# Row sums of attention: one pair of slabs added on VectorE, two chained to it on POOL, half the sums on TensorE

## The reference

```
h = _sln(hidden, w, ...)                       # layer norm, gain and bias from w
qkv = (h @ Wqkv.T + bqkv).reshape(B, N, num_heads, hd, 3)
energy = jnp.einsum('bhqd,bhkd->bhqk', q, k)
att = jax.nn.softmax(energy, axis=-1) / D ** 0.5
out = jnp.einsum('bhqk,bhkd->bhqd', att, v)
out = out.reshape(B, N, D) @ Wp.T + bp
h1 = out + hidden
return _sln(h1, w, ...) + h1
```

## Time and profile before

| | |
|---|---|
| median of three runs | 1395.69 us |
| the profiled execution | 1395.35 us |
| its span | 1393.7 us |
| mean granted clock of TensorE | 0.979 |
| PE busy | 1331.2 us, 96% |
| DVE busy | 909.3 us, 65% |
| ACT busy | 701.5 us, 50% |
| POOL busy | 984.6 us, 71% |
| sums on PE (L864), busy, both buffers | 110.9 + 16.8 us |
| adds on POOL (L1642), busy, both buffers | 493.4 + 75.7 us |

### The profile page before, as it was taken

How to read it: one execution, slowest core, us unless ns; L and a number is a source line. 1 busy time by engine, 2 the same in 40 slices (tenths; PEclk the granted TensorE clock), 3 DMA queues, 4 the chain that set the end, 5 groups by cost and what they waited for, 6 DMA issues and landing times.

```text
span 1393.7 us, 34891 instructions
## 1 busy us (share of the span) xinstructions
PE 1331.2 (96%) x10948; PEld 928.2 (67%) x10948; DVE 909.3 (65%) x1634; ACT 701.5 (50%) x1374; POOL 984.6 (71%) x755
## 2 busy tenths in 40 slices
PE   6898999999999999999999999999999999999993
PEld 4897676767676767777676767677656555655562
DVE  5345767667676767676776767666666667666535
ACT  4221455555555555555555555555564646565341
POOL 1443175656666688979787888877797969797845
PEclk8899899999999999999999999999999999999997
DMA  7577534443443545645453544626463424253321
GB/s 245 155 209 221 131 93 108 111 106 116 106 115 86 151 107 144 154 124 147 113 159 88 165 118 140 155 77 165 103 168 85 116 80 119 83 137 92 87 56 64
DMA packets 216709, 174.17 MB, mean 125 GB/s; under 512 B 105492, under 2 KB 186516, under 8 KB 216632
## 3 DMA queue, kind: packets, MB, share of 16 engines
q1 hardware_dynamic: 214456, 166.83, 44.7%
q0 software_dynamic: 1984, 6.29, 1.2%
q10 hardware_dynamic: 192, 0.07, 0.0%
HBM read 113.29 MB, written 58.51 MB: 123 GB/s over the span
## 4 chain that ended last, share of the span: by engine, by line
PE 83%; DVE 5%; SPq 4%; issue 3%; DMA 2%; ACT 1%; POOL 1%; DVEq 1%; POOLq 0%; ACTq 0%
PE ps_o L851 15%; PE ps_st L834 15%; PE ps_a L820 12%; PE ps_w L725 10%; PE ps_w L783 9%; PE ps_s L864 8%; PE ps_st L820 4%; PE ps_st L783 3%; DVE half_max L1360 3%; PE ps_w L898 1%; PE ps_w L771 1%; PE ps_s L876 1%; PE ps_s L783 1%; PE ps_o L725 1%; ACT p L1129 1%
## 5 line engine op out<-in xcount | busy, mean ns | idle before, releaser
L1129 ACT ACTIVATE p<-ps_st 128x512 f32<-128x512 f32 x864 | 484.7, 600 | 436.9 <-PE ps_st L834 433.1
L1360 DVE TENSOR_REDUCE half_max<-ps_a 128x1 f32<-128x512 f32 x729 | 484.6, 685 | 256.4 <-PE ps_a L820 254.1
L1642 POOL TENSOR_TENSOR p<-p 128x1024 f32<-128x1024 f32 x208 | 493.4, 2392 | 220.2 <-PE ps_o L851 219.3
L834 PE MATMUL ps_st<-q_stack,k_stack 98*128 98x512 f32 x1024 | 415.7, 408 | 8.4 <-DMA q_stack<-max_rows 4.6
L820 PE MATMUL ps_a<-k_stack,q_stack 96*128 96x512 f32 x729 | 305.8, 421 | 12.7 <-DVE half_max L1360 10.0
L834 PEld LDWEIGHTS ps_st<-q_stack,k_stack 98*128 98x128 f32 x1024 | 195.1, 191 | 72.9 <-ACT p L1129 38.0
L851 PE MATMUL ps_o<-p,v_head 128*32 128x256 f32 x3456 | 209.2, 382 | 0.0
L1360 DVE TENSOR_REDUCE half_max<-ps_st 128x1 f32<-128x512 f32 x231 | 158.3, 685 | 70.7 <-PE ps_st L820 70.7
L820 PEld LDWEIGHTS ps_a<-k_stack,q_stack 96*128 96x128 f32 x729 | 138.0, 190 | 88.0 <-issue 40.8
L783 PEld LDWEIGHTS ps_w<-hT_s,wqkv_s 128*128 128x128 f32 x1056 | 157.2, 190 | 20.1
L851 PEld LDWEIGHTS ps_o<-p,v_head 128*32 128x32 f32 x3456 | 110.1, 110 | 78.4 <-issue 5.0
(11 more groups left out here) (199 smaller groups left out, 1361.7 us busy)
## 6 DMA issues: line engine op xcount, KB each, us to landing
qk_scratch<-qkT_s SPq DMA_DIRECT2D x108, 256.0 KB, 2.4
q_stack<-qk_scratch SPq DMA_DIRECT2D x192, 128.0 KB, 2.6
k_stack<-qk_scratch SPq DMA_DIRECT2D x192, 128.0 KB, 2.8
x_tile<-in_x SPq DMA_DIRECT2D x34, 256.0 KB, 4.9
gq_s<-gain_bias_scratch SPq DMA_DIRECT2D x16, 512.0 KB, 4.3
v_scratch<-v_parts SPq DMA_DIRECT2D x32, 256.0 KB, 3.3
v_head<-v_scratch SPq DMA_DIRECT2D x64, 128.0 KB, 2.1
att_scratch<-o_stage SPq DMA_DIRECT2D x240, 32.0 KB, 1.5
```

The costliest lines, as they stand in the source:

```text
L834: pe.matmul(ps_st[:, (ST_BANK_WIDE if wide else ST_BANK)[2 * k + e], :], k_stack[0:98, s, k * 128:(k + 1) * 128], q_stack[0:98, s, e * 512 ...
L1129: nc.scalar.activation(p_of(step // 8, tiles)[:, k, e * 512:(e + 1) * 512], ps_st[:, (ST_BANK_WIDE if tiles else ST_BANK)[2 * k + e], :], ...
L1360: V.tensor_reduce(half_max[:, s % 2, item:item + 1], A_BANK[bank], AX.X, ALU.max).then_inc(a_used, 1)
L1642: G.tensor_tensor(p[:, slot, :], p[:, slot - 2, :], p[:, slot, :], ALU.add).then_inc(pair_added, 1)
```

## The change

Per half head there were two adds on POOL and two groups of sums on PE. Now the slabs 4h, 4h+1, 4h+2, 4h+3 of half h are joined to one. DVE adds slab 4h to 4h+1 (`slab_add`), when PE's weighted part has read these two (the count of `pv_done` after the first two slabs of the block). POOL adds 4h+2 to 4h+3, when all four are read, and then 4h+1 to 4h+3, when DVE's add and its own first one are done. PE sums slab 3 and slab 7 alone (`chain_sum`). POOL's number of adds stays. `sum_done` counts two a head instead of four.

DVE's adds stand in its order at step 0 (second half of the head before) and at step 4 (first half), behind the reductions, the evacuation and the negated maxima of that step, and ahead of the rest. ACT's waits follow: slab 0 and 4 are free after DVE's add, 2 and 6 after POOL's first, 1 and 5 after POOL's second, 3 and 7 after the sum.

```diff
-        SUM_SLOT = [2, 3, 6, 7]
+        SUM_SLOT = [3, 7]
...
-            def pair_sums(g, s, j, near=False):
+            def chain_sum(g, s, h, near=False):
...
-                pe.wait_ge(pair_added, 16 * g + 4 * s + j + 1)
+                pe.wait_ge(pair_added, 16 * g + 4 * s + 2 * h + 2)
                 for e in range(4):
-                    mm = pe.matmul(ps_s[HD * e:HD * e + HD, 0:QW], root_s[:], p_of(s, near)[:, SUM_SLOT[j], e * QW:(e + 1) * QW],
-                                   start=(j == 0), stop=(j == 3))
+                    mm = pe.matmul(ps_s[HD * e:HD * e + HD, 0:QW], root_s[:], p_of(s, near)[:, SUM_SLOT[h], e * QW:(e + 1) * QW],
+                                   start=(h == 0), stop=(h == 1))
...
-                j = 2 * (k // 4) + k % 2 if paired else k // 2
-                freed = 16 * i + 4 * (step // 8) + j + 1 - 4 * behind
+                half, v = k // 4, 4 * i + step // 8 - behind
+                freed, count = {0: (slab_added, 2 * v + half + 1), 1: (pair_added, 4 * v + 2 * half + 2),
+                                2: (pair_added, 4 * v + 2 * half + 1), 3: (sum_done, 2 * v + half + 1)}[k % 4 if paired else 3]
...
+            def slab_add(g, s, h, near):
+
+                dve.wait_ge(pv_done, 16 * g + 4 * s + 2 * h + 1)
+                p = p_of(s, near)
+                V.tensor_tensor(p[:, 4 * h + 1, :], p[:, 4 * h, :], p[:, 4 * h + 1, :], ALU.add).then_inc(slab_added, 1)
...
+                        if k == 0 and not (first and s == 0) and not (last and s > 0):
+                            slab_add(i - (s == 0), (s - 1) % 4, 1, tiles or (joining and s == 0))
+                        if k == 4 and not last:
+                            slab_add(i, s, 0, tiles)
...
             def pair_add(g, s, j, near=False):
...
+                if j % 2:
+                    pool.wait_ge(slab_added, 8 * g + 2 * s + h + 1)
+                    pool.wait_ge(pair_added, total + j)
+                else:
+                    pool.wait_ge(pv_done, total + 2 * h + 2)
+                G.tensor_tensor(p[:, 4 * h + 3, :], p[:, 4 * h + 2 - j % 2, :], p[:, 4 * h + 3, :], ALU.add).then_inc(pair_added, 1)
```

More of the change, by code:

```diff
@@ L218, in conditioned_attention @@
         pv_done = sem("pv_done")
+        slab_added = sem("slab_added")
         pair_added = sem("pair_added")
@@ L877, in slab_sums @@
                                        start=(k == 0), stop=(k == 7))
-                mm.then_inc(sum_done, 1)
+                if j % 2:
+                    mm.then_inc(sum_done, 1)
             def fin_part(n):
@@ L993, in iteration @@
                                     weighted(*before, j, near=near)
-                            for j in (0, 1):
-                                pair_sums(*before, j, near=near)
+                            chain_sum(*before, 0, near=near)
                             if mode != "bare":
@@ L1002, in iteration @@
                         if k == 4 and behind and (not last or finishing):
-                            for j in (2, 3):
-                                pair_sums(*before, j, near=near)
+                            chain_sum(*before, 1, near=near)
                         if k == 4 and tiles:
@@ L1105, in take_sums @@
             def take_sums(v, s):
-                act.wait_ge(sum_done, 4 * v + 4)
+                act.wait_ge(sum_done, 2 * v + 2)
                 nc.scalar.activation(o_stage[:, s % 2, QW:2 * QW], ps_s[:, 0:QW], ACT.Copy).then_inc(s_taken, 1)
@@ L1126, in exps @@
                     if e == 0:
-                        need(act, pair_added if paired and k not in SUM_SLOT else sum_done, freed)
+                        need(act, freed, count)
                     nc.scalar.activation(p_of(step // 8, tiles)[:, k, e * 512:(e + 1) * 512], ps_st[:, (ST_BANK_WIDE if tiles else ST_BANK)[2 * k + e], :], ACT.Exp
@@ L1319, in last_norm @@
                 dve.wait_ge(pv_done, 4 * NV)
-                dve.wait_ge(sum_done, 4 * NV)
+                dve.wait_ge(sum_done, 2 * NV)
                 dve.wait_ge(att_out[1], ATT_LAST)
@@ L1403, in _, with iteration @@
                     tile_stats(LEAD, step // 3)
-            def iteration(i, mode, norms, outs, first=False, late=True, closing=False):
+            def iteration(i, mode, norms, outs, first=False, late=True, closing=False, joining=False):
                 pair = i - FIRST_OUTS
@@ L1462, in _ @@
             iteration(LAST_TILES - 1, "tiles", False, True)
-            with dve.Fori(LAST_TILES, LAST - 1) as i:
+            iteration(LAST_TILES, "bare", False, True, joining=True)
+            with dve.Fori(LAST_TILES + 1, LAST - 1) as i:
                 iteration(i, "bare", False, True)
@@ L1637, in pair_add @@
             def pair_add(g, s, j, near=False):
-                slot = SUM_SLOT[j]
-                pool.wait_ge(pv_done, 16 * g + 4 * s + 2 * (j // 2) + 2)
+                h, total = j // 2, 16 * g + 4 * s
                 p = p_of(s, near)
-                G.tensor_tensor(p[:, slot, :], p[:, slot - 2, :], p[:, slot, :], ALU.add).then_inc(pair_added, 1)
+                if j % 2:
+                    pool.wait_ge(slab_added, 8 * g + 2 * s + h + 1)
[3 more added lines that the diff above has]
+                G.tensor_tensor(p[:, 4 * h + 3, :], p[:, 4 * h + 2 - j % 2, :], p[:, 4 * h + 3, :], ALU.add).then_inc(pair_added, 1)
             def norm(pair, a):
```

2 lines of the change are left out of this document (1 added, 1 removed).

## The result

The changed kernel takes 1387.26 us (median of four runs, 1385.82 to 1391.84), the kernel before 1395.99 on the same chip: ratio 0.9942, interval 0.9917 to 0.9966. Six more runs gave 1386.39 (e11), ratio 0.9928, interval 0.9913 to 0.9943. The profile called after is of the slowest execution of its four (1391.84), that of e11 of the fastest of its six (1382.51). I had forecast 1402 and slower; it is 0.6% to 0.7% faster. The time lies in the range, but the direction is wrong. It is my second rival (1384) that came about.

A forecast was written before the change was run, and what follows sets the result against it. PE was taken to bound iterations 0 to 9, POOL's path 11 to 14; -15.6 + 0 - 2.9 + 15.7 = -2.8, plus 4 (DVE) and 5 (clock), gave +6: 1402 us, range 1370 to 1418.

The forecast's parts named there:

- my second rival (1384): Whole kernel not slower: POOL loses nearer 0.8 than 1.1 us per add, waits 35 us, giving 1384; chance 0.25.
- PE's gain, 53 us: On PE, each of 120 blocks loses one of two groups of sums, 0.443 us each, 53.2 us in all.
- The exclusion: A DVE op with two SBUF inputs and a POOL op do not run together; whichever comes second waits.
- The loss per add, "where POOL is busy, it loses the full 1.1": Where POOL has no idle time before its adds, each DVE add costs it 1.1 us.
- the turning point at 0.95 a loss: About 0.95 us of POOL loss per add decides between not slower and slower.
- Iterations 5 to 9, forecast 0: POOL's lag adds up; PE waits 3.6 us an iteration against a gain of 3.5: nothing, five times.
- Iterations 11 to 14, forecast +15.7: POOL is level with PE already; PE waits 29.9 us against a gain of 14.2, net loss 15.7.
- the 5 us that I gave the clock: New PE waits in iterations 11 to 14 bring one or two clock falls, 5 us in sum, between none and 12.
- DVE's own waits, +4: DVE waits for POOL's op (0.7 to 1.1 us) in six tight half heads, about 0.7 each, 4 us.
- Iterations 0 to 3, forecast -3.1 each: DVE goes first, POOL starts 0.35 us late; one sum in eight comes 0.4 late, gain 3.1 an iteration.
- +0.4 (10): Iteration 10: PE has one wait of 0.6 us, leaving a gain of 2.9.

The follow-up runs named there:

- e11: The changed kernel unaltered, measured once more in six runs: 1386.39 us, ratio 0.9928 to the kernel before.
- e1: Changed kernel with DVE's add replaced by a reduction of the same length with one SBUF input (slab 4h missing from sums): 1359.61 us, ratio 0.973.
- e2: Changed kernel with no DVE instruction in the add's place, only the count passed on (slab 4h missing from sums): 1362.29 us, ratio 0.9747.
- e3: Changed kernel with POOL's second add of each half left out, DVE's add kept (two slabs missing from sums): 1354.38 us, ratio 0.9696.
- e4: Changed kernel with each group of sums done twice on PE, giving back the removed work: 1429.7 us, ratio 1.0237.
- e9: Changed kernel, but with the form before in iterations 11 to 14 and in three half heads of iterations 5 to 9: 1371.37 us, ratio 0.9822.
- e7: Changed kernel with DVE's add over 512 of the 1024 columns (the other half missing from the sum): 1377.18 us, ratio 0.9866.
- e8: Changed kernel with the form before in three half heads from iteration 4, and in 11 to 14 except three half heads: 1387.74 us, ratio 0.993.
- e10: Changed kernel with DVE's add moved ahead of the reductions of its step: 1603.48 us, ratio 1.148.

## Why the prediction was wrong

**PE's gain, 53 us: right.** Where nothing else holds PE, e1 gives 3.66 us for each of iterations 6 to 8, e2 and e3 3.4, the forecast 3.54.

**The exclusion: right.** What I read from instructions of 256 elements holds at 1024: e1 against the change shows it, and each collision shown here has the same arithmetic. POOL and DVE in iteration 6 after the change:

```profile
616.98 1.29 POOL L1562 TENSOR_TENSOR y_t<-y_t,go_s 128x512 f32<-128x512 f32 x1
618.28 5.79 POOL L1658 TENSOR_TENSOR p<-p 128x1024 f32<-128x1024 f32 x2
...
628.03 1.51 POOL L1549 TENSOR_TENSOR res_t<-res_t,bp_s 128x512 f32<-128x512 f32 x1
...
635.71 0.77 POOL L1523 TENSOR_SCALAR h_tile<-x_tile,std_t 128x512 f32<-128x512 f32 x1 [0.20 <-issue]
636.66 2.04 POOL L1531 TENSOR_TENSOR h_tile<-h_tile,gq_s 128x512 f32<-128x512 f32 x1 [0.18 <-POOL h_tile L1523]
...
646.54 1.58 POOL L1514 TENSOR_TENSOR std_t<-std_t,minus_half 128x1 f32<-128x1 f32 x1
```
```profile
617.73 1.63 DVE L1294 TENSOR_TENSOR p<-p 128x1024 f32<-128x1024 f32 x1
...
627.16 1.22 DVE L1294 TENSOR_TENSOR p<-p 128x1024 f32<-128x1024 f32 x1
...
635.98 1.57 DVE L1294 TENSOR_TENSOR p<-p 128x1024 f32<-128x1024 f32 x1 [0.36 <-PE ps_o L852]
...
646.49 1.23 DVE L1294 TENSOR_TENSOR p<-p 128x1024 f32<-128x1024 f32 x1 [0.78 <-PE ps_o L852]
```

At 617.73 DVE waits for POOL's 1.29 us and ends at 619.36, 1.09 after it; POOL's pair of adds then lasts 5.79 in place of 4.75. Undisturbed, the add took 1.22, the size that I took.

The Trainium skill (SBUF — State Buffer, section Who interferes with whom) says that a DVE instruction with two SBUF inputs contends with a POOL instruction that reads SBUF, and that this sharing is an exclusive lock: one holds it and the other blocks. e1 and the change agree with it, 1359.6 against 1387.3 us. Which of the two blocks is not told by the starts of their records: in e4 DVE's stands first (642.42 against 642.61), and DVE was blocked.

**The loss per add, "where POOL is busy, it loses the full 1.1": the step that failed.** Of the four adds shown above, the first costs POOL 1.0, the second 0.2 (1.51 against 1.29: most of DVE's time lay beside POOL's pause and its DMA), the third 0.8, the fourth 1.0, and that on an instruction of one column (1.58 where its likes take 0.56). The mean over the run is 0.65, and 0.65 over the eight adds of an iteration like this one too (71.39 against the 66.18 us that POOL is busy in iteration 6 of e1). In iteration 13, where it matters most, it is 0.77 (63.34 against 57.18 in iteration 12 before). I had seen POOL's pauses and read them as too short to help (0.68 at most), but the part of an add that lies beside a pause costs POOL nothing, as the second of the four shows. The prediction itself put the turning point at 0.95 a loss; 0.65 and 0.77 lie below it. The rival's own figures were not hit in their parts: PE's waits are 30.8 us where it had 35, and the clock, by the estimate below, took some 6 where it had 2, so that 1384 is met in part by luck.

**Iterations 5 to 9, forecast 0, came out at -1.6 each.** PE's idle time rose from 0.55 (the 79.22 less 78.67 of the earlier trace rows) to 2.13 us, 1.6 in place of my 3.6 of waits.

**Iterations 11 to 14, forecast +15.7, came out at +14.5 and +11.6.** The waits before the sums are 19.0 us in e11 (four of 3.3 to 3.5 for p_far, four of 1.2 to 1.4 for p), where I had 29.9, for the same reason. Less the 14.2 us of fewer sums that makes 4.8 of the 11.6. Most of the other 6.8 is the clock, by the estimate below. (In the prediction I wrote that PE had idled 3.0 us at 1113.08; the row has 2.59.) POOL, PE and the windows there, e11:

```profile
1148.81 3.21 POOL L1658 TENSOR_TENSOR p_far<-p_far 128x1024 f32<-128x1024 f32 x1
```
```profile
1152.08 1.08 PE L865 MATMUL ps_s<-p_far,root_s 128*32 128x256 f32 x8 [3.49 <-POOL p_far L1658]
...
1154.11 0.63 PE L821 MATMUL ps_a<-k_stack,q_stack 96*128 96x512 f32 x1
...
1158.02 0.40 PE L821 MATMUL ps_a<-k_stack,q_stack 96*128 96x512 f32 x1
```
```profile
1152.08:1157.52 5.44, 5.44 (x18) 3.67 (x19) 2.95 (x5) 2.65 (x5) 5.36 (x4) 0.50 0.94 190
1157.52:1166.02 8.50, 8.11 (x63) 4.72 (x61) 8.20 (x14) 6.32 (x13) 8.42 (x5) 1.00 0.20 55
```

PE had idled 3.49 us, and the 5.4 us behind ran at 0.50 (1.2 GHz), products of 512 columns at 0.63 us, then at 1.00 (2.4 GHz) and 0.40. One such stretch holds ten products that start 0.43 us apart in place of 0.24, and eight sums that take 1.0 in place of 0.5: about 2.5 us, an estimate from these rows. Iterations 11, 13 and 14 each have one of these and 12 one half as long (1082.5 to 1085.9); before only 12 had one. That is 2.5 more than before, some 6 us. So the 5 us that I gave the clock were about right, and were needed inside the 11.6. That of iteration 11 may not be the change's own, as e9 shows.

**DVE's own waits, +4: 2 to 3 at most.** The waits of PE's weight loads for the reductions are 36.8 us against 34.6 in e1, where POOL blocks no instruction of DVE's; PE's own are 11.9 against 11.5. e4, e7 and e8 show when this term is real: when several instructions of POOL pass DVE's add.

**Iterations 0 to 3, forecast -3.1 each, came out at -2.3.** I had let DVE go first and POOL start 0.35 late. But the add stands behind reductions that run until 1.1 to 2.0 us after the weighted part's start, so DVE was late and blocked POOL's first add. PE, POOL and DVE in iteration 1:

```profile
362.07 0.64 PE L865 MATMUL ps_s<-p,root_s 128*32 128x256 f32 x8
370.06 0.64 PE L865 MATMUL ps_s<-p,root_s 128*32 128x256 f32 x8 [0.65 <-POOL p L1658]
```
```profile
364.55 5.45 POOL L1658 TENSOR_TENSOR p<-p 128x1024 f32<-128x1024 f32 x2 [2.78 <-PE ps_o L852]
```
```profile
364.08 1.22 DVE L1294 TENSOR_TENSOR p<-p 128x1024 f32<-128x1024 f32 x1
```

The pair lasts 5.45 where the earlier trace rows have 4.72. ACT's exponentials, which wait for POOL's second add, wait 37.7 us in the run, 2.3 before. In e1 these waits are 7.1 us and the iterations gain 3.4, in e7 4.3 us and 3.1. That the loss passes through these waits fits both, but no run singles it out. So this part was counted too well, by 3.4 us in all.

**The sum.** From forecast to e11, by the table: -7.6 (5 to 9), -4.1 (11 to 14), -5 (the clock's place outside), -4 (DVE), +3.4 (0 to 4), +0.4 (10): from +6 to -10.9, to within rounding. The rest of the difference lies ahead of the first block, which starts 2.6 us earlier in e11 and 2.4 later in the first profile of after, which I did not look into.

What stays open: how much of iterations 11 to 14 in e3 the transfers and the clock explain, why iteration 11 differs so much from run to run, and by what rule a waiting DVE is or isn't served between two instructions of POOL (after one at 617.73, only after three at 1166.81, after two in e4 and e7).

## What to carry to other kernels

A saving on the bounding engine that is paid with an add on a neighbour must be priced stretch by stretch: here it gained 1.6 to 3.2 us an iteration in 0 to 4 and 6 to 10, where POOL had pauses or slack, and cost 4.4 and 4.7 in 13 and 14, where POOL was level with PE (12 gained 0.8, and 11 is not clear). Where two engines exclude each other, price a collision by the overlap that really occurs, not by the whole instruction, and first ask whether one SBUF input would do. The place of an instruction that waits matters more than its length: what stands behind it waits too (217 us in e10), and where it starts in the other engine's order decides who blocks whom (e4, e7, e8).

## What the hardware showed that I had not expected

- DVE's 128x1024 instruction with one input in SBUF beside POOL's adds costs neither anything (1215 and 2391 ns); with two inputs POOL's adds rise to 2558 ns in the mean.
- A POOL instruction of 128x1, 0.56 us alone, took 1.58 behind DVE's add: smallness does not protect it.
- A blocked DVE add can be passed by several POOL instructions: 5.70 us instead of 1.22 in e8, 4.92 in e4, and 4.18 instead of 0.69 for the half width of e7.
- The blocked time stands inside the record of the blocked instruction, so a busy share can rise (POOL 71% to 76%) with no work added.
